# Graph attention: value aggregation one quad later and split between the score products, K|V buffers returned tile by tile

## The chip, the core and the metric

The kernel runs on one core of a Trainium2 chip. The metric is the device time of one execution in microseconds (us). TensorE does the matrix products (PE in the profile, its weight loads PEld), VectorE is DVE, ScalarE is ACT, GpSimd is POOL and SyncE is SP. The DMA engines move data between memory (HBM) and the on-chip buffers, and they are started here by SP (plain copies) and by POOL (gathers and scatters by index).

## The reference, cut to what matters

A graph of 3125 nodes with 512 features and 53125 edges, sorted by target node. After a layer norm the kernel computes two graph-attention layers, a linear-attention branch on the same input, and a mixture of eight small feed-forward experts. The change touches the attention over edges, which runs once in each of the two layers:

```python
q = ((x @ Wq[l].T + bq[l]) * scaling).reshape(n, H, DH)     # H = 8 heads, DH = 64
k = (x @ Wk[l].T).reshape(n, H, DH)
v = (x @ Wv[l].T).reshape(n, H, DH)
scores = jnp.einsum('ehd,ehd->eh', q[tgt], k[srcidx])
m = segment_max(scores, tgt); p = jnp.exp(scores - m[tgt]); s = segment_sum(p, tgt)
agg = segment_sum((p / (s[tgt] + 1e-16))[:, :, None] * v[srcidx], tgt)
```

## The kernel before

**Tiles, quads, groups.** The edges are padded to 416 tiles (`ET`) of 128. Four tiles are a quad, 104 quads (`NQ`); two quads are a group of eight tiles, 52 groups (`NJ`). Within a tile at most 16 different target nodes occur (`CAP` slots), and eight heads times 16 slots give 128 columns.

**What one quad needs.** POOL gathers, for every tile, the 128 rows of K|V (4 KB each, 512 KB in all) by source index into one of `KVN` = 20 buffers in layer 0 and 25 in layer 1 (`fetch`, line 1096). For every group it gathers the Q rows (`fetch_slots`, line 1105) and writes the 128 aggregated rows back by index (`scatter`, line 1113). So POOL starts five indexed DMAs in a quad: four `fetch`, and a `fetch_slots` or a `scatter` in turn. All are issued one after another on the one POOL queue, in the order of the program, and each waits for its semaphores there.

TensorE, per iteration `g` of the loop in `attend_pe`:

1. `turn_k` (line 1179): transposes K of four tiles, two ahead (`LOOK`), four 128x128 transposes for a tile. It waits for the tile's K|V DMA. ACT (line 1346) and DVE (line 1284) copy the results out of PSUM.
2. `turn_hot` (line 1160) in even iterations, `turn_q` (line 1171) in odd ones.
3. `turn_p` (line 1186): transposes the probabilities of quad `g - 2`; DVE copies them into `probs` (line 1272).
4. `masks` (line 1197): four bf16 products that start the score bank of the quad.
5. `score` (line 1209) for four tiles: for each tile four products, each with 32 weight columns, into partitions 0 to 31, 32 to 63, 64 to 95 and 96 to 127 (the columns of the array in four strips). The last one of a tile increments the semaphore `sc`. After the fourth tile DVE takes the minimum over the bank (line 1277) and ACT the exponentials (line 1365, one iteration later).
6. `gather` (line 1221) of quad `g - AGG_AT`, `AGG_AT` = 2: for each of the eight heads a product for each of the four tiles, with 32 weight columns from `probs` and V of the tile as the moving operand. Tile `i` goes to strip `i` of the bank `AG`. The very last product increments `agg`.

The profile's records show a product of fp32 operands in `score` and `gather` as two, so 32 records of line 1209 and 64 of line 1221 stand for a quad.

**What `agg` releases.** POOL's `fetch` of tile `n` waits until the quad that holds tile `n - KVN` is aggregated; `empty_p` on DVE waits for it before it overwrites `probs`; `empty_agg` on DVE (line 1297), once for a group, copies the bank `AG` out, increments `ev`, and `scatter` waits for `ev`. In layer 0 TensorE, DVE and ACT also do the output of the linear-attention branch in between (`side`; lines 743 to 796 on TensorE and DVE): these generators are advanced at four points of an iteration, and none lies between `score` and `gather`. Layer 1 has no such side work.

The order of the instructions on every engine is fixed by these loops and by the list that `turn_table` writes; nothing is reordered by a planner.

Of the kernel before, what the change touches and what calls it, by code (L numbers as in the profile page):

```python
# [7 lines left out]
N, D, H, DH = 3125, 512, 8, 64  # L8
# [5 lines left out]
ET = 416  # L14
# [14 lines left out]
LOOK = (2, 2)  # L29
AGG_AT = 2  # L30
FAR = 8192.0
# [49 lines left out]
def build(nc, A, out):  # L81
    with ExitStack() as ctx:
# [744 lines left out]
        def turn_table(l):  # L827
# [3 lines left out]
            for g in range(NQ + AGG_AT):  # L831
                b, x = divmod(g, 2)
                order += [("k", n) for n in range(4 * g + LOOK[l], 4 * g + LOOK[l] + 4) if n < ET]
                if x == 0 and b + 2 < NJ:
                    order.append(("hot", b + 2))
                if x == 1 and b + 1 < NJ:
                    order.append(("q", b + 1))
                if g >= AGG_AT:
                    order.append(("p", g - AGG_AT))
            place, by, count = {}, [], {"a": 0, "d": 0}  # L840
# [14 lines left out]
        def place_of(l, kind, n):  # L855
            return TURNED_AT[l][0][kind, n]
# [227 lines left out]
        def attend_pool(l, begin):  # L1084
# [7 lines left out]
            def fetch(n):  # L1092
                a = n % KV
                if n >= KV:
                    pool.wait_ge(agg, NQ * l + (n - KV) // 4 + 1)
                pool.indirect_dma_start(out=kvs[a], out_offset=None, in_=KVd[l][:, :],  # L1096
# [36 lines left out]
            at = KV  # L1133
            for g in range(NQ + AGG_AT + 2):
                j = (g + 3) // 2
                if g % 2 and j < NJ:
                    fetch_slots(j)
                x = (g - 2 - AGG_AT) // 2
                if g % 2 == AGG_AT % 2 and 0 <= x < NJ:
                    scatter(x)  # L1140
                while at < ET and (at - KV) // 4 <= g - AGG_AT:
                    fetch(at)
                    at += 1

        def attend_pe(l, side):
# [66 lines left out]

            def gather(g):
                x = g % 2
                is_emptied(pe, l, place_of(l, "p", g))
                if x == 0 and g:
                    pe.wait_ge(ev, NJ * l + g // 2)
                for h in range(H):
                    for i in range(4):
                        a = (4 * g + i) % KVN[l]  # L1220
                        mm = pe.matmul(AG[32 * i:32 * i + 32, DH * h:DH * (h + 1)], probs[x][:, i, h, :],  # L1221
                                       kvs[a][:, D + DH * h:D + DH * (h + 1)], start=(x == 0 and h == 0), stop=(x == 1),
                                       skip_group_check=True)
                mm.then_inc(agg, 1)
# [11 lines left out]
            for g in range(NQ + AGG_AT):  # L1236
# [9 lines left out]
                if x == 1 and b + 1 < NJ:  # L1246
                    turn_q(b + 1)
                if g >= AGG_AT:
                    turn_p(g - AGG_AT)
                next(side, None)  # L1250
                if g < NQ:
                    masks(g)
                    for i in range(4):
                        score(4 * g + i)
                if g >= AGG_AT:
                    gather(g - AGG_AT)
                next(side, None)

        def attend_dve(l, side, begin, work_free):
# [7 lines left out]
            def empty_p(g):  # L1267
                x = g % 2
                bank = bank_of("p", g)
                if g >= 2:  # L1270
                    dve.wait_ge(agg, NQ * l + g - 1)
                dve.tensor_copy(probs[x][:, :, :, CAP * x:CAP * (x + 1)],  # L1272
# [20 lines left out]
            def empty_agg(j):  # L1293
                dve.wait_ge(agg, NQ * l + 2 * j + 2)
                if j or l:
# [20 lines left out]
            for g in range(NQ + AGG_AT):  # L1316
# [5 lines left out]
                if x == 0 and b + 2 < NJ:  # L1322
                    empty_hot(l, b + 2)
                if g >= AGG_AT:
                    empty_p(g - AGG_AT)
                next(side, None)
# [62 lines left out]
        def edges_done(e, l):  # L1389
            e.wait_ge(agg, NQ * (l + 1))  # L1390
            e.wait_ge(ev, NJ * (l + 1))
# [1267 lines left out]
```

## Time and profile before

| | |
|---|---|
| median of 3 runs | 3487.64 us (3484.23 to 3498.01) |
| profiled execution | 3486.91 us, span 3485.6 us |
| PE busy | 2825.2 us (81%) |
| PEld busy | 2291.8 us (66%) |
| DVE, ACT, POOL busy | 1626.5, 1323.0, 1161.3 us (47%, 38%, 33%) |
| chain that ended last | PE 75%, issue 12%, DVE 8%, DMA 2%, ACT 2% |
| mean granted TensorE clock | 0.918 of full speed |

A record of a matmul has a start that is measured and an end that is modelled. "issue" is time in which an engine waited for nothing that the profile can name, and "remote" is a releaser that it can't name. Attention of layer 0 lies at about 512 to 1425 us of the span, that of layer 1 at about 1880 to 2781 us.

### The profile page before, as it was taken

The page shows a single profiled execution, that of the slowest core. Times are in us where ns is not written, and L with a number is a line of the kernel's source. Part 1 is how long each engine was busy: PE and PEld are TensorE (multiplying, and loading weights), DVE is VectorE, ACT ScalarE, POOL GpSimd, SP SyncE. Part 2 cuts the span into 40 slices and gives each one's busy share as a digit, 9 for nine tenths or more (in the row PEclk, how much of TensorE's full clock was granted, in tenths as well). Part 3 has the DMA queues.
Part 4 walks back from the last instruction along what each step waited for, and adds up shares of the span by engine and source line. Part 5 has one row for each costly group of instructions (what it writes and reads, how often), then busy time and mean ns, then how long its engine had stood idle before and what let it go on. Part 6 is the DMA issues. An engine that isn't in the chain of part 4 may idle for free.

```text
span 3485.6 us, 78342 instructions
## 1 busy us (share of the span) xinstructions
PE 2825.2 (81%) x32605; PEld 2291.8 (66%) x32605; DVE 1626.5 (47%) x3272; ACT 1323.0 (38%) x3690; POOL 1161.3 (33%) x1130
## 2 busy tenths in 40 slices
PE   6999978888888888587996777777777758588888
PEld 5877866666676676464885666666666646366676
DVE  5247764444444444547123333333443455655443
ACT  3324434444444444322322344444444412243333
POOL 0000015555555555100012555655565401312110
PEclk8999989999999999789998899998988979799989
DMA  6531037887888888430234777777777642022211
GB/s 215 218 139 68 28 127 237 264 268 264 269 269 273 266 270 270 109 117 0 91 148 147 253 260 263 268 261 258 264 261 259 184 114 72 25 78 89 64 52 53
DMA packets 231795, 621.75 MB, mean 178 GB/s; under 512 B 39008, under 2 KB 45792, under 8 KB 231427
## 3 DMA queue, kind: packets, MB, share of 16 engines
q0 software_dynamic: 137088, 466.78, 40.1%
q1 hardware_dynamic: 94339, 149.78, 12.9%
q8 instruction: 265, 4.34, 0.5%
q14 instruction: 103, 0.84, 0.1%
HBM read 538.80 MB, written 103.39 MB: 184 GB/s over the span
## 4 chain that ended last, share of the span: by engine, by line
PE 75%; issue 12%; DVE 8%; DMA 2%; ACT 2%; another core or an unknown queue 1%; POOL 0%; SPq 0%; POOLq 0%; DVEq 0%; ACTq 0%
PE ps L1179 12%; PE ps L1221 9%; PE ps L1209 6%; PE ps L574 4%; PE ps L576 4%; PE ps L575 4%; PE ps L1186 3%; PE ps L774 3%; PE ps L942 2%; PE ps L944 2%; PE ps L943 2%; PE ps L1867 2%; PE ps L1171 1%; PE ps L1869 1%; PE ps L1868 1%
## 5 line engine op out<-in xcount | busy, mean ns | idle before, releaser
L1096 POOL DMA_INDIRECT Y<-KVd,srcE x449 | 457.2, 1018 | 374.9 <-PE ps L1221 237.8
L1277 DVE TENSOR_REDUCE stage<-ps 128x4 f32<-128x512 f32 x208 | 143.8, 692 | 629.8 <-remote 501.1
L1346 ACT ACTIVATE work<-ps 128x512 f32<-128x512 f32 x309 | 179.7, 597 | 506.8 <-PE ps L1179 472.3
L1221 PE MATMUL ps<-Y,G 128*32 128x64 f32 x7184 | 237.7, 226 | 161.9 <-issue 158.9
L1346 ACT ACTIVATE G<-ps 128x512 f32<-128x512 f32 x315 | 182.1, 598 | 421.8 <-PE ps L1179 388.4
L1096 POOL DMA_INDIRECT WA<-KVd,srcE x186 | 188.6, 1014 | 419.4 <-PE ps L576 266.3
L1221 PEld LDWEIGHTS ps<-Y,G 128*32 128x32 f32 x7184 | 181.9, 112 | 207.2 <-issue 202.7
L1365 ACT ACTIVATE stage<-ps,stage 128x128 f32<-128x128 f32 x832 | 294.0, 366 | 35.0 <-PE ps L1186 27.1
L1179 PE MATMUL ps<-ident,Y 128*128 128x128 f32 x1796 | 261.3, 303 | 2.6 <-issue 1.4
L574 PE MATMUL ps<-Wh,xs 128*128 128x512 f32 x600 | 239.0, 398 | 29.9 <-DVE xs L514 29.8
L1179 PEld LDWEIGHTS ps<-ident,Y 128*128 128x128 f32 x1796 | 231.9, 158 | 29.3 <-issue 21.0
L576 PE MATMUL ps<-Wh,xs 128*128 128x512 f32 x600 | 236.7, 395 | 0.0
L575 PE MATMUL ps<-Wl,xs 128*128 128x512 f32 x600 | 236.5, 394 | 0.0
L1272 DVE COPY G<-ps 128x512 f32<-128x512 f32 x208 | 143.8, 691 | 165.3 <-PE ps L1186 136.0
L1105 POOL DMA_INDIRECT stage<-Qd,segs x104 | 105.9, 1018 | 330.8 <-DVE segs L893 195.3
L514 DVE TENSOR_TENSOR xs<-xT,xs 128x512 fp32r<-128x512 f32 (+1 forms) x100 | 67.8, 679 | 235.3 <-ACT xs L539 235.3
L1096 POOL DMA_INDIRECT mt<-KVd,srcE x54 | 53.8, 997 | 357.4 <-DMA Qd<-stage 319.7
L1365 ACT ACTIVATION_READ_ACCUMULATOR stage<-ps,stage 128x1 f32 x832 | 169.2, 203 | 0.0
L1221 PE MATMUL ps<-WA,G 128*32 128x64 f32 x2976 | 101.2, 230 | 68.4 <-issue 67.3
L574 PEld LDWEIGHTS ps<-Wh,xs 128*128 128x128 f32 x600 | 113.1, 188 | 56.5 <-issue 23.2
L1291 DVE TENSOR_TENSOR stage<-stage,st 128x512 f32<-128x512 f32 x208 | 143.9, 692 | 7.1
L2567 PE MATMUL ps<-W2hi,workR 128*128 128x512 f32 (+1 forms) x200 | 94.6, 473 | 58.4 <-DVE mtR L2614 58.4
(383 smaller groups left out, 6950.0 us busy)
## 6 DMA issues: line engine op xcount, KB each, us to landing
KVd<-stage SPq DMA_DIRECT2D x96, 256.0 KB, 2.0
aggd<-work SPq DMA_DIRECT2D x6, 2048.0 KB, 7.4
Qd<-stage SPq DMA_DIRECT2D x48, 256.0 KB, 2.0
G<-aggd SPq DMA_DIRECT2D x48, 256.0 KB, 2.7
Y<-KVd,srcE POOLq DMA_INDIRECT x449
Y<-in_x SPq DMA_DIRECT2D x4, 1536.0 KB, 15.0
G<-mixq SPq DMA_DIRECT2D x24, 256.0 KB
mixd<-rowsb SPq DMA_DIRECT2D x24, 256.0 KB
```

Of the source, the lines that this page charges most:

```text
L574: pe.matmul(PS[e % 4][0:r, :], xh, Wh[:, w, k, :], start=(k == 0), stop=False)
L575: pe.matmul(PS[e % 4][0:r, :], xh, Wl[:, w, k, :], start=False, stop=False)
L576: mm = pe.matmul(PS[e % 4][0:r, :], xl, Wh[:, w, k, :], start=False, stop=(k == 3))
L1096: pool.indirect_dma_start(out=kvs[a], out_offset=None, in_=KVd[l][:, :], in_offset=bass.IndirectOffsetOnAxis(ap=srcE[:, n:n + 1], axis=0)) ...
L1179: mm = pe.transpose(bank[:, k * P:(k + 1) * P], kvs[a][:, k * P:(k + 1) * P], ident[:, :])
L1209: mm = pe.matmul(bank[32 * k:32 * k + 32, at], qblk[j % 2][:, k, 2 * (c % 4) + c // 4, :], kT[n % len(kT)][:, k * P:(k + 1) * P], start=Fa ...
L1221: mm = pe.matmul(AG[32 * i:32 * i + 32, DH * h:DH * (h + 1)], probs[x][:, i, h, :], kvs[a][:, D + DH * h:D + DH * (h + 1)], start=(x == 0 ...
L1272: dve.tensor_copy(probs[x][:, :, :, CAP * x:CAP * (x + 1)], bank[:, :].rearrange("p (c h s) -> p c h s", c=4, h=H)).then_inc(out_d, 1)
L1277: dve.tensor_reduce(smin[:, 4 * g:4 * g + 4], SC[g % 2][:, :].rearrange("p (c e) -> p c e", c=4), AXX, ALU.min).then_inc(mins, 1)
L1291: dve.tensor_tensor(p4, p4, rec4[:, :].unsqueeze(2).to_broadcast([P, 4, P]), ALU.mult).then_inc(normed, 1)
L1346: act.activation(kT[n % len(kT)], banks(l)[place_of(l, "k", n) % len(banks(l))][:, :], ACT.Copy).then_inc(out_a, 1)
L1365: last = act.activation(pT[g % len(pT)][:, P * i:P * (i + 1)], SC[g % 2][:, P * i:P * (i + 1)], ACT.Exp, bias=smin[:, t:t + 1], scale=-1.0 ...
```

## The change

`gather` takes the tile as a second argument. It now does the eight products of one tile and increments `agg` once for every tile. The loop of TensorE calls it behind each `score`, so an iteration does score, gather, score, gather and so on; and the quad that is aggregated is the one three back (`AGG_AT` = 3), while its probabilities are still transposed two iterations after the scores (`P_AT` = 2). Every wait on `agg` counts tiles instead of quads. `fetch` of tile `n` waits for tile `n - KVN` alone. In POOL's loop `scatter` now stands ahead of `fetch_slots`, and with `AGG_AT` odd both fall into the odd iterations. The loops have one more iteration in each attention. The number of products, copies and DMAs is the same.

```diff
--- before.py
+++ after.py
@@ -27,7 +27,7 @@
 CAP = 16
 MASK = 2.0 ** 100
 LOOK = (2, 2)
-AGG_AT = 2
+P_AT, AGG_AT = 2, 3
 FAR = 8192.0
 BIG = 1.0e30
 EPS = 1e-5
@@ -835,8 +835,8 @@
                     order.append(("hot", b + 2))
                 if x == 1 and b + 1 < NJ:
                     order.append(("q", b + 1))
-                if g >= AGG_AT:
-                    order.append(("p", g - AGG_AT))
+                if 0 <= g - P_AT < NQ:
+                    order.append(("p", g - P_AT))
             place, by, count = {}, [], {"a": 0, "d": 0}
             for e, (kind, n) in enumerate(order):
                 who = "d" if kind in ("hot", "p") or kind == "k" and n % 4 == K_DVE[l] else "a"
@@ -1092,7 +1092,7 @@
             def fetch(n):
                 a = n % KV
                 if n >= KV:
-                    pool.wait_ge(agg, NQ * l + (n - KV) // 4 + 1)
+                    pool.wait_ge(agg, ET * l + n - KV + 1)
                 pool.indirect_dma_start(out=kvs[a], out_offset=None, in_=KVd[l][:, :],
                                         in_offset=bass.IndirectOffsetOnAxis(ap=srcE[:, n:n + 1], axis=0)
                                         ).then_inc(kv_in[a], 16)
@@ -1132,12 +1132,12 @@
                 fetch(n)
             at = KV
             for g in range(NQ + AGG_AT + 2):
+                x = (g - 2 - AGG_AT) // 2
+                if g % 2 == AGG_AT % 2 and 0 <= x < NJ:
+                    scatter(x)
                 j = (g + 3) // 2
                 if g % 2 and j < NJ:
                     fetch_slots(j)
-                x = (g - 2 - AGG_AT) // 2
-                if g % 2 == AGG_AT % 2 and 0 <= x < NJ:
-                    scatter(x)
                 while at < ET and (at - KV) // 4 <= g - AGG_AT:
                     fetch(at)
                     at += 1
@@ -1210,17 +1210,16 @@
                                    kT[n % len(kT)][:, k * P:(k + 1) * P], start=False, stop=True, skip_group_check=True)
                 mm.then_inc(sc, 1)
 
-            def gather(g):
-                x = g % 2
-                is_emptied(pe, l, place_of(l, "p", g))
-                if x == 0 and g:
-                    pe.wait_ge(ev, NJ * l + g // 2)
+            def gather(g, i):
+                x, a = g % 2, (4 * g + i) % KVN[l]
+                if i == 0:
+                    is_emptied(pe, l, place_of(l, "p", g))
+                    if x == 0 and g:
+                        pe.wait_ge(ev, NJ * l + g // 2)
                 for h in range(H):
-                    for i in range(4):
-                        a = (4 * g + i) % KVN[l]
-                        mm = pe.matmul(AG[32 * i:32 * i + 32, DH * h:DH * (h + 1)], probs[x][:, i, h, :],
-                                       kvs[a][:, D + DH * h:D + DH * (h + 1)], start=(x == 0 and h == 0), stop=(x == 1),
-                                       skip_group_check=True)
+                    mm = pe.matmul(AG[32 * i:32 * i + 32, DH * h:DH * (h + 1)], probs[x][:, i, h, :],
+                                   kvs[a][:, D + DH * h:D + DH * (h + 1)], start=(x == 0 and h == 0), stop=(x == 1),
+                                   skip_group_check=True)
                 mm.then_inc(agg, 1)
 
             if l == 0:
@@ -1245,15 +1244,16 @@
                     turn_hot(b + 2)
                 if x == 1 and b + 1 < NJ:
                     turn_q(b + 1)
-                if g >= AGG_AT:
-                    turn_p(g - AGG_AT)
+                if 0 <= g - P_AT < NQ:
+                    turn_p(g - P_AT)
                 next(side, None)
                 if g < NQ:
                     masks(g)
-                    for i in range(4):
+                for i in range(4):
+                    if g < NQ:
                         score(4 * g + i)
-                if g >= AGG_AT:
-                    gather(g - AGG_AT)
+                    if g >= AGG_AT:
+                        gather(g - AGG_AT, i)
                 next(side, None)
 
         def attend_dve(l, side, begin, work_free):
@@ -1268,7 +1268,7 @@
                 x = g % 2
                 bank = bank_of("p", g)
                 if g >= 2:
-                    dve.wait_ge(agg, NQ * l + g - 1)
+                    dve.wait_ge(agg, ET * l + 4 * (g - 1))
                 dve.tensor_copy(probs[x][:, :, :, CAP * x:CAP * (x + 1)],
                                 bank[:, :].rearrange("p (c h s) -> p c h s", c=4, h=H)).then_inc(out_d, 1)
 
@@ -1291,7 +1291,7 @@
                 dve.tensor_tensor(p4, p4, rec4[:, :].unsqueeze(2).to_broadcast([P, 4, P]), ALU.mult).then_inc(normed, 1)
 
             def empty_agg(j):
-                dve.wait_ge(agg, NQ * l + 2 * j + 2)
+                dve.wait_ge(agg, ET * l + 4 * (2 * j + 2))
                 if j or l:
                     dve.wait_ge(sct, 16 * (NJ * l + j))
                 dve.tensor_copy(stage[:, 0, :], AG[:, :]).then_inc(ev, 1)
@@ -1321,8 +1321,8 @@
                 next(side, None)
                 if x == 0 and b + 2 < NJ:
                     empty_hot(l, b + 2)
-                if g >= AGG_AT:
-                    empty_p(g - AGG_AT)
+                if 0 <= g - P_AT < NQ:
+                    empty_p(g - P_AT)
                 next(side, None)
                 if g < NQ:
                     least(g)
@@ -1387,7 +1387,7 @@
                 next(side, None)
 
         def edges_done(e, l):
-            e.wait_ge(agg, NQ * (l + 1))
+            e.wait_ge(agg, ET * (l + 1))
             e.wait_ge(ev, NJ * (l + 1))
 
         def edges_stored(e, l):
```

## Rows read from the trace of the kernel before

**Rows 1.** Windows: attention of layer 0 and of layer 1, and the opening of layer 1's.

```profile
core 0: us, PE busy (x) PEld busy (x) DVE busy (x) ACT busy (x) POOL busy (x), PEclk, DMA share, GB/s
520.00:1385.00 865.00, 731.12 (x12807) 594.99 (x12805) 396.05 (x883) 391.06 (x1227) 494.82 (x481) 0.97 0.80 265
1920.00:2757.00 837.00, 634.48 (x11881) 561.14 (x11874) 327.33 (x630) 363.66 (x1163) 488.24 (x484) 0.89 0.78 260
...
1886.90:1902.30 15.40, 5.37 (x32) 2.65 (x22) 0.29 (x1) 0.52 (x1) 9.47 (x11) 0.66 1.00 380
```

**Rows 2.** Chain of waits in layer 1, two quads: start us, us, what.

```profile
2182.16 3.51 PE ps L1179 x16
...
2186.44 1.01 PE ps L1209 x32
...
2189.71 1.02 PE ps L1221 x55
2190.74 1.90 PE ps L1179 x16
...
2193.73 1.01 PE ps L1209 x32
...
2198.29 0.91 PE ps L1221 x47
2199.19 0.40 PE ps L1179
```

**Rows 3.** Timeline of POOL over the same two quads.

```profile
2182.44 1.30 POOL L1096 DMA_INDIRECT rowsb<-KVd,srcE  x1 [2.13 <-PE ps L1221]
...
2187.77 1.00 POOL L1113 DMA_INDIRECT aggd<-stage,segs  x1 [0.30 <-issue]
2191.01 1.29 POOL L1096 DMA_INDIRECT WA<-KVd,srcE  x1 [2.24 <-PE ps L1221]
...
2196.33 1.02 POOL L1105 DMA_INDIRECT stage<-Qd,segs  x1 [0.30 <-issue]
```

**Rows 4.** Timeline of DVE over the same two quads.

```profile
2189.97 0.69 DVE L1277 TENSOR_REDUCE stage<-ps 128x4 f32<-128x512 f32 x1 [3.03 <-remote]
```

**Rows 5.** Chain of waits near the end of layer 1's attention, no fetches left.

```profile
2763.56 1.01 PE ps L1209 x32
2764.57 0.89 PE ps L1221 x64
2765.47 1.90 PE ps L1179 x16
...
2769.24 0.11 issue
```

**Rows 6.** Timeline of POOL near the end of layer 1's attention.

```profile
2768.05 0.99 POOL L1113 DMA_INDIRECT aggd<-stage,segs  x1 [10.88 <-DVE stage L1297]
```

**Rows 7.** Timelines of POOL and of DVE, opening of layer 1's attention.

```profile
1886.06 0.94 POOL L1096 DMA_INDIRECT Y<-KVd,srcE  x1 [0.31 <-issue]
...
1898.48 0.94 POOL L1096 DMA_INDIRECT rowsb<-KVd,srcE  x1 [0.31 <-issue]
...
1902.62 0.69 DVE L1277 TENSOR_REDUCE stage<-ps 128x4 f32<-128x512 f32 x1 [14.12 <-remote]
```

**Rows 8.** Chain of waits in layer 0, first and last row of four quads.

```profile
1005.25 1.01 PE ps L1209 x32
...
1039.94 0.23 PE ps L1209
```

**Rows 9.** Windows: the rest of these four quads, outside score and gather, summed.

```profile
sum 19.35, PE 18.73 PEld 15.28 DVE 10.98 ACT 9.86 POOL 14.47; mean PE 4.68 PEld 3.82 DVE 2.75 ACT 2.46 POOL 3.62
```

**Rows 10.** Chain of waits at the end of layer 0's attention.

```profile
1405.76 7.09 DMA Y<-KVd,srcE
```

**Rows 11.** Chain of waits in layer 0, a change from score to gather.

```profile
927.52 0.04 PE ps L1221 x3
927.56 0.01 PE ps L1209
927.57 0.94 PE ps L1221 x60
```

## The prediction, made before the run

> **What bounds the kernel now.** I read the page first and then split the span into stretches; both attentions together are half of it. In layer 0 and in layer 1 alike PE is busy for 85% and 76% of the time, DMA for 80% and 78%, POOL for 57% and 58% [rows 1]. None of them is full, so the bound is a loop. The chain of waits shows it. In layer 1 two quads take 2199.19 - 2182.16 = 17.03 us, 8.52 us a quad, and the 32 records of the scores are through in 1.01 us, but the mass of the gather follows only 2.3 and 3.6 us later, with PE waiting for nothing the profile can name [rows 2]. The stall is real, not one of recording: DVE, which needs only the last score, starts its minimum at 2189.97, 0.26 us after the gather moves again [rows 4].
>
> The timeline of POOL tells what the stall follows. A train of five indexed DMAs starts at 2182.44 and its last issue ends at 2188.77; PE moves again at 2189.71, 0.94 us behind it. The next train starts at 2191.01 and ends at 2197.35; PE moves at 2198.29, again 0.94 us behind [rows 2, 3]. From the first issue to the release are 7.27 and 7.28 us, 1.455 us for each DMA. Two counterproofs stand in the same trace. Near the end, where no fetch is left, the scores and the gather of a quad take 2765.47 - 2763.56 = 1.91 us and there is no stall; one lone scatter issued at 2768.05 ends a little stall that lasts to 2769.35, 1.30 us from its issue [rows 5, 6]. At the opening of layer 1, POOL issues eleven fetches in a row from 1886.06, and DVE waits 14.12 us for the first quad's scores, until 1902.62: 16.56 us, 1.51 us for each DMA [rows 7]. So products on 32-column strips (scores and gather) hardly complete while POOL issues indexed DMAs, whereas the transposes of line 1179 go on beside them: 16 in 1.90 us, the pace of the quad without fetches [rows 2, 5].
>
> The loop of a quad is therefore: gather done, 0.27 us, five DMAs at 1.455 us each (7.27), release, the rest of the scores and the gather (about 0.95), together 8.5 us. The transposes lie under the train. Layer 0 runs at (1039.94 - 1005.25) / 4 = 8.67 us a quad [rows 8].
>
> **The change part by part.** Products, copies and DMAs are the same in number, so only waits move. A release by tile lets POOL start its train inside the stretch of scores and gathers, where the train does its harm.
>
> (a) Layer 1. Let PE be free to work on strips at T. A tile's score and gather take 1.91 / 4 = 0.48 us [rows 5]. POOL's first fetch starts at T + 0.48 + 0.27 = T + 0.75. How soon it stops PE the trace bounds: not before 0, and behind the lone scatter PE still took in records until 2769.24, 1.19 us after its issue [rows 5, 6]; I take 0.5 us, nearer to 0 because records are queued before they are executed. By T + 1.25 two to three tiles are gathered, and their fetches make a train of three: 3 x 1.455 = 4.37, release at T + 5.12. The fourth tile ends at T + 5.60. The rest of the quad (transposes and masks) takes 2193.73 - 2190.74 = 2.99 and 2186.44 - 2182.16 = 4.28 us, the second at the lower granted clock; mean 3.64 [rows 2]. Sum 9.24 us. The fourth fetch lies under that rest. In every second iteration scatter and slots come behind it: 0.27 + 3 x 1.455 = 4.64 us, 1.0 more than the rest covers, 0.5 a quad. Together 9.75 us against 8.52: +1.23 us, times 104 quads +128 us.
>
> (b) Layer 0, the same loop. The rest of a quad is 19.35 / 4 = 4.84 us because of the side work [rows 9], which covers those three DMAs: 5.60 + 4.84 = 10.44 us.
>
> (c) Layer 0, K|V buffers. With 20 of them and the gather three back, buffers free after iteration g - 1 allow fetches up to tile 4g + 7, and `turn_k` of iteration g wants tile 4g + 5 at once (with two back: 4g + 11). So the second fetch released by one iteration is needed at the start of the next. It is issued 0.75 + 1.30 + 0.30 = 2.35 us after T [rows 3]; the chain shows 7.09 us from such an issue to the data [rows 10], so tile 4g + 5 can be turned at T + 9.44. Its transposes (1.90 / 4 = 0.48) and what follows them until the scores (2.99 - 1.90 = 1.09) [rows 2] come behind: 11.0 us. Bounds: 7.09 was behind other fetches, so 11.0 is an upper end; the lower end is nothing, where 10.44 of (b) stays. I take 10.6 us: 10.6 - 8.67 = +1.93, times 104 quads +201 us. In layer 1 with 25 buffers the allowance is 4g + 12, seven tiles to spare, no cost.
>
> (d) Taken away: the gather no longer waits for DVE's copy of the same iteration's probabilities. That copy runs beside the scores, and the stall behind them is longer than it; worth nothing. POOL's new order puts `scatter` and `fetch_slots` behind one another: the wait of `fetch_slots` for `turn_q` now has nothing behind the scatter to fill it, and the fetches of the iteration stand behind it in POOL's queue; they need gathers that come later anyway. Between 0 and one DMA (1.455 us) in every second quad of layer 0, where side work makes `turn_q` late; I take 0 and keep 52 x 1.455 = 76 us for the range. `empty_agg` and `ev` move with the gather and are awaited an iteration's transposes later: nothing.
>
> (e) One more iteration in each attention and a first refill one quad later: about 4 us each, +8 us, an estimate from half a quad; between 0 and 2 x 9.
>
> Sum: 128 + 201 + 8 = +337 us. The profiled execution took 3486.91 us (span 3485.6), within 1 us of the median, 3487.64. 3487 + 337 = 3824; I say 3825 us.
>
> **Rules of the skill.** The row first: near 927.5 us three records of the gather stand ahead of the last record of the scores [rows 11], so products on other strips pass one that is held, and I let the eight products of one tile, all on one strip, overlap with the next tile's scores. The Trainium skill ("TensorE: Matmul & The Clock Gate", Part 3: Packing small matmuls) says that matmuls start and end strictly in program order. By that rule they would run one behind another, the serial rival below. The skill ("SBUF — State Buffer", SBUF: two separate sides) also says that engine ports and DMA ports can't disturb each other and that TensorE waits for nobody there. By that the stall would have another cause, and the faster rival below would be the likelier. Rows 7 speak against it.
>
> **Rivals.**
>
> Serial strips. A tile's 16 gather records on one strip take as long as 64 on four, 0.89 us [rows 5], so a tile costs 0.89 + 0.25 = 1.14. After a gather PE has 0.27 + 0.5 us before the fetch stops it, less than a tile: every tile pays its own DMA. The next tile does 0.77 of its 1.14 us, waits for the release 0.27 + 1.455 = 1.73 after that gather and ends 0.37 later: 2.1 us a tile, the fourth at T + 7.4. A quad takes 7.4 + 3.64 + 0.5 = 11.5 us in layer 1 (+3.0) and 7.4 + 4.84 = 12.2 in layer 0 (+3.6), 104 x 6.6 = 686 us: 4170 us. For it speaks that the products are on one strip; against it rows 11.
>
> Faster: POOL's issues don't stop PE when strip work comes in small pieces. Then layer 1 is bound by POOL's train, five issues, 2196.33 + 1.02 + 0.30 - 2191.01 = 6.64 us a quad [rows 3]: -1.88 x 104 = -196 us. Layer 0 keeps (c), whose loop without the stall is 0.48 + 0.27 + 1.60 + 7.09 + 1.57 = 11.0 us at most and what it is now at least: 0 to +240, middle +100 (nearer to the lower end, since 7.09 is an upper one). About 3390 us. It decides if a quad's strip work in layer 1 ends less than about 3 us after it began although POOL is issuing. Against it: every one of the trains above.
>
> Same: the fetches collect into one train as before and the data of (c) arrive early; 3495 us.
>
> Only (c): the stall is no longer than before in either layer and only layer 0 pays: 3487 + 201 = 3690 us.
>
> **How the numbers follow.** The loop of (a) to (c) 0.50, serial strips 0.20, only (c) 0.07, same 0.09, faster 0.14. The likeliest gives 3825 us, its own range 3640 (onset at 1.2 us, so that all tiles are through in layer 1) to 4000 (76 us of (d), and a lower clock for the transposes in every quad, 104 x 0.9). The range given goes down to 3470, which takes in the same case, and up to 4250, which takes in the serial strips: outside it are the faster case (0.14) and a few hundredths above. Half a per cent, 17 us, is about what a measurement of this kernel can tell from no change; faster by more than that 0.14, within it 0.09, slower 0.77.
>
> **What the profile after would show.** If right: two stalls in each iteration between records of lines 1209 and 1221, each about 0.9 us behind the end of a POOL issue; POOL idle before fetches twice in a quad rather than once, with 1221 as releaser; about 9.7 us a quad in layer 1 and 10.6 in layer 0, there with line 1179 waiting for K|V DMAs; DMA in layer 1 at 260 x 8.52 / 9.75 = 227 GB/s. Serial strips would show as 16 records of line 1221 spread over 0.9 us even where POOL is idle. The prediction is wrong if the strips' work proceeds beside POOL's issues: a quad of layer 1 then falls below 8 us.

## The result and the profile after

Before 3492.82 us (median of 4 runs, 3484.23 to 3501.8), after 3780.09 us (4 runs, 3769.35 to 3783.95): 1.0817 times, 95% interval 1.0779 to 1.0856. The change makes the kernel 287 us slower, +8%; predicted were 3825 us (3470 to 4250). The profiled execution took 3769.35 us, its span is 3768.0 us, 282 more than the span before.

Where the time went is quickly told by line 1197, of which each quad has four products: the first and the last start of its rows, 103 quads apart, give the mean quad. Here is the view of line 1197 by attention, of before and then of after (count, durations, first and last start in us):

```profile
L1197 PE MATMUL ps<-hotTs,maskA x416: 216/219/229, 520.3 to 1417.6; 128*128 128x128 bf16 x139
L1197 PE MATMUL ps<-hotTs,maskA x416: 219/219/311, 1886.0 to 2771.8; 128*128 128x128 bf16 x139
```

```profile
L1197 PE MATMUL ps<-hotTs,maskA x416: 218/219/315, 520.5 to 1665.4; 128*128 128x128 bf16 x139
L1197 PE MATMUL ps<-hotTs,maskA x416: 218/219/314, 2139.9 to 3044.0; 128*128 128x128 bf16 x139
```

Layer 0 goes from 8.71 to 11.12 us a quad, 104 x 2.41 = 250 us; layer 1 from 8.60 to 8.78, 104 x 0.18 = 19 us. The rest, 13 us, lies around the attentions. So nearly all of it is layer 0, while I had expected 128 us of it in layer 1.

The page after, to set beside the table of before, and its windows, one for each attention (columns as in [rows 1]):

```profile
PE 3184.1 (85%) x32605; PEld 2662.0 (71%) x32605; DVE 1612.9 (43%) x3272; ACT 1317.1 (35%) x3690; POOL 1127.9 (30%) x1130
...
PE 60%; DMA 12%; DVE 10%; another core or an unknown queue 8%; issue 5%; ACT 2%; POOL 1%; SPq 1%; DVEq 0%; POOLq 0%; ACTq 0%
```

```profile
520.00:1664.00 1144.00, 971.70 (x13296) 845.41 (x13296) 404.71 (x907) 413.64 (x1274) 489.82 (x495) 0.96 0.64 207
2140.00:3043.00 903.00, 794.89 (x12403) 711.44 (x12402) 332.61 (x658) 370.73 (x1227) 491.69 (x501) 0.99 0.78 252
```

PE is busy for 359 us more than the 2825.2 of before, with the same 32605 records: the same work is now wider in time. DMA stands in the chain with 12% instead of 2%. (The 8% with an unnamed releaser lie mostly in layer 1; the piece at 2203.79, 6.43 us long, is DVE's minimum waiting for the scores of its quad.) In layer 0 the chain of waits shows why (start us, us, what):

```profile
1011.33 0.35 PE ps L1209 x8
1011.68 0.82 PE ps L1220 x15
...
1014.52 0.26 issue
1014.77 5.37 DMA Y<-KVd,srcE
...
1020.29 1.08 PE ps L1179 x4
...
1022.76 1.71 PE ps L774 x2
...
1028.79 5.37 DMA Y<-KVd,srcE
...
1034.29 0.63 PE ps L1179 x4
...
1039.15 5.56 DMA Y<-KVd,srcE
```

One turn of the loop is read off it: the second tile's gather ends at 1014.52, 0.26 us later its fetch starts, 5.37 us later the data are there, the transposes of that one tile, the side work (line 774) and the rest follow, then the scores and two gathers, and the next fetch of the same kind starts at 1028.79, 14.02 us after the last. The next turn takes 10.36 us. That is step (c) of the prediction. It does not bind every turn: from 530 to 1640 us, about 100 turns, the chain passes through 67 such DMAs (median 5.45 us), and the mean turn is 11.12 us. Two more things are to be seen. Fifteen or sixteen records of line 1220 take 0.82 to 0.9 us each time, as long as the 64 of a whole quad before, 0.89 us [rows 5]: the products of one strip run one behind another, 0.056 us apart. And behind the first of these waits PE works at the lower clock: four transposes take 1.08 us there and 0.63 in the second turn. The windows give the granted clock in the last column but two, 0.50 of full speed (the 1.2 GHz level). This is the rare case: over layer 0 the mean is 0.96, against 0.97 before [rows 1]. The window behind the first wait:

```profile
1020.30:1024.80 4.50, 4.50 (x17) 3.10 (x17) 1.31 (x5) 2.10 (x9) 0.00 (x0) 0.50 0.32 127
```

In layer 1 PE waits for no K|V data. The timeline of PE (start us, us, line, count, idle before) over most of a quad, and that of POOL:

```profile
2203.18 1.00 PE L1220 MATMUL ps<-Y,G 128*32 128x64 f32 x15
...
2205.10 0.80 PE L1209 MATMUL ps<-work,qblk 128*32 128x128 f32 x6
2206.22 0.40 PE L1220 MATMUL ps<-Y,G 128*32 128x64 f32 x4 [0.32 <-issue]
2206.98 0.46 PE L1220 MATMUL ps<-Y,G 128*32 128x64 f32 x5 [0.35 <-issue]
2207.70 0.38 PE L1220 MATMUL ps<-Y,G 128*32 128x64 f32 x4 [0.26 <-issue]
...
2208.23 1.06 PE L1220 MATMUL ps<-Y,G 128*32 128x64 f32 x16
```

```profile
2201.59 1.21 POOL L1096 DMA_INDIRECT Y<-KVd,srcE  x1 [1.04 <-PE ps L1220]
2203.40 1.01 POOL L1113 DMA_INDIRECT aggd<-stage,segs  x1 [0.60 <-PE ps L1186]
2204.71 1.03 POOL L1105 DMA_INDIRECT stage<-Qd,segs  x1 [0.30 <-issue]
2206.05 0.96 POOL L1096 DMA_INDIRECT Y<-KVd,srcE  x1 [0.31 <-issue]
```

The stall is there, but it is not a full stop: from 2206.22 to 2208 the products come four or five at a time, 0.72 to 0.76 us apart. And POOL's issues stand in shorter trains. If an idle time over 0.5 us is counted as a break, layer 1 of before (1920 to 2757 us) has 96 trains, each of five, as in [rows 3]; after (2180 to 3000 us) it has 183 single issues, 65 trains of two, 49 of three and one of five.

### The profile page after: what moved, and what is told of

The parts are those of the page before. It is cut to its first block, busy times and chain, and to the rows that moved or that the text cites. A ratio compares the mean times of both kernels' runs of the same rounds, so it can differ in the third digit from the quotient of the medians.

```text
span 3768.0 us, 78342 instructions
## 1 busy us (share of the span) xinstructions
PE 3184.1 (85%) x32605; PEld 2662.0 (71%) x32605; DVE 1612.9 (43%) x3272; ACT 1317.1 (35%) x3690; POOL 1127.9 (30%) x1130
## 4 chain that ended last, share of the span: by engine, by line
PE 60%; DMA 12%; DVE 10%; another core or an unknown queue 8%; issue 5%; ACT 2%; POOL 1%; SPq 1%; DVEq 0%; POOLq 0%; ACTq 0%
PE ps L1220 11%; DMA Y<-KVd,srcE 6%; PE ps L1179 5%; PE ps L1209 5%; PE ps L574 4%; PE ps L575 4%; PE ps L576 4%; PE ps L1186 3%; DMA G<-KVd,srcE 2%; PE ps L942 2%; PE ps L944 2%; PE ps L943 2%; DMA WA<-KVd,srcE 2%; PE ps L774 2%
## 5 line engine op out<-in xcount | busy, mean ns | idle before, releaser
L1096 POOL DMA_INDIRECT Y<-KVd,srcE x449 | 438.0, 976 | 499.2 <-PE ps L1220 325.8
L1220 PE MATMUL ps<-Y,G 128*32 128x64 f32 x7184 | 487.6, 221 | 31.3 <-issue 30.4
L1220 PEld LDWEIGHTS ps<-Y,G 128*32 128x32 f32 x7184 | 455.1, 112 | 49.5 <-issue 48.5
L1179 PE MATMUL ps<-ident,Y 128*128 128x128 f32 x1796 | 243.0, 278 | 90.8 <-DMA Y<-KVd,srcE 80.2
L1179 PEld LDWEIGHTS ps<-ident,Y 128*128 128x128 f32 x1796 | 199.6, 143 | 132.3 <-issue 76.7
L1220 PE MATMUL ps<-WA,G 128*32 128x64 f32 x2976 | 200.6, 220 | 13.3 <-issue 13.0
L1220 PEld LDWEIGHTS ps<-WA,G 128*32 128x32 f32 x2976 | 187.5, 111 | 19.1 <-issue 18.9
L1186 PE MATMUL ps<-ident,stage 128*128 128x128 f32 x832 | 137.8, 291 | 26.9 <-ACT G L1346 7.0
```

The source lines that it names most:

```text
L1179: mm = pe.transpose(bank[:, k * P:(k + 1) * P], kvs[a][:, k * P:(k + 1) * P], ident[:, :])
L1186: mm = pe.transpose(bank[:, i * P:(i + 1) * P], pT[g % len(pT)][:, i * P:(i + 1) * P], ident[:, :])
```

## The experiments

The kernels ran in three groups, each beside runs of the kernel before on the same chip: e1 to e4 (before: 3131.65 us), e5 to e8 (3473.49 us), e9 to e12 (3492.54 us). The first group's chip ran the kernel before 10% faster than the others; what was seen of that chip is told in the last section. us a quad is read from line 1197 as above. The first group's chip has no profile of before; its layer 0 stands in e2 (7.39 us) and its layer 1, unchanged, in e1 (6.45).

| kernel | times before, interval | layer 0, us a quad | layer 1 |
|---|---|---|---|
| e1 before, 16 buffers in layer 0 | 1.173, 1.168 to 1.177 | 12.70 | 6.45 |
| e2 after, layer 0 as before | 1.026, 1.021 to 1.030 | 7.39 | 7.16 |
| e3 three back, whole | 1.172, 1.167 to 1.177 | 12.61 | 6.44 |
| e4 three back, parts by heads | 1.168, 1.163 to 1.173 | 12.48 | 6.43 |
| e5 before | 1.000, 0.998 to 1.002 | 8.60 | 8.53 |
| e6 after | 1.083, 1.080 to 1.087 | 11.26 | 8.67 |
| e7 two back, parts by tile | 1.053, 1.050 to 1.057 | 10.26 | 8.61 |
| e8 two back, parts by heads | 1.029, 1.026 to 1.032 | 9.00 | 9.06 |
| e9 two back, tile by tile at the end | 1.060, 1.056 to 1.063 | 10.11 | 9.13 |
| e10 after, 20 buffers in layer 1 | 1.141, 1.138 to 1.143 | 11.22 | 10.73 |
| e11 before, half rows | 0.994, 0.992 to 0.996 | 8.61 | 8.53 |
| e12 after, release by quad | 1.253, 1.249 to 1.256 | 15.08 | 10.65 |

### The look-ahead alone: e1, e3, e4, e10

e1, on the kernel before:

```diff
-KVN = (20, 25)
+KVN = (16, 25)
```

> The kernel before with 16 instead of 20 K|V buffers in layer 0: same order, same products, but the same look-ahead as after the change (buffers free after iteration g-1 allow fetches up to tile 4g+7). Theory supply (layer 0's loss is the short look-ahead, the data of tile 4g+5 come too late): the release comes at the end of the gather, the second fetch is issued 0.27 + 1.27 us later, its data 5.4 us after that, then transposes, side work, masks, scores and gather (about 5 us): 12 us a quad instead of 8.7 in layer 0, 3490 + 104 x 3.3 = 3830 us. Rival order (layer 0's loss comes from products in series on one strip and from the stalls that they meet): nothing of that is changed here, 3490 us.

Measured 3675.36 us, 12.70 us a quad in layer 0 against 7.39: +5.3. The products, their order and the number of DMAs are those of before; only the look-ahead is that of after. Two turns in e1's chain of waits:

```profile
1195.38 5.37 DMA Y<-KVd,srcE
...
1209.06 5.13 DMA WA<-KVd,srcE
...
1219.86 0.90 POOL G L1096
1220.76 0.45 issue
1221.21 5.30 DMA G<-KVd,srcE
```

The turns take 13.68 and 12.15 us, of which 5.1 to 5.4 are a fetch's way from issue to data; in the second, 1.35 more are the first fetch, which stands ahead of the one that is needed. The expectation had been reckoned on the slower chip's time before. The quad came out near it, 12.70 for 12 us, but the loss did not: +5.3 us for +3.3, 1.173 times for 1.10.

A part of the 5.3 us is the clock. Layer 0 without and with the short look-ahead on this chip, e2 and then e3, which loses as e1 does:

```profile
530.00:1270.00 740.00, 671.09 (x13011) 570.04 (x13009) 402.23 (x890) 395.74 (x1245) 479.99 (x492) 0.98 0.89 314
530.00:1800.00 1270.00, 843.56 (x12944) 687.95 (x12943) 405.63 (x889) 406.26 (x1242) 494.18 (x490) 0.80 0.55 183
```

The mean granted clock is 0.80 instead of 0.98, and PE is busy for 843.56 instead of 671.09 us with about as many records (12944 and 13011). That is 1.7 us more a quad (1.8 in e1): PE waits for data, and then does the same work at the lower clock for part of the time.

e3 and e4, on the kernel after. e3:

```diff
                     if g < NQ:
                         score(4 * g + i)
-                    if g >= AGG_AT:
-                        gather(g - AGG_AT, i)
+                if g >= AGG_AT:
+                    gather_whole(g - AGG_AT)    # the loop over h, then i, of before; agg += 4
```

> The kernel after, but the gather stands whole at the end of the iteration, heads outermost (four strips in turn); it is still the quad three back. Theory supply: layer 0 has the look-ahead of e1 and its late release, 12 us a quad: 3830 us; layer 1 as before, 8.5. Rival order: without one-strip series both layers are as before, 3490 us.

e4:

```diff
-                for h in range(H):
-                    mm = pe.matmul(AG[32 * i:32 * i + 32, ...], probs[x][:, i, h, :], kvs[a][...], ...)
-                mm.then_inc(agg, 1)
+                for h in (2 * i, 2 * i + 1):
+                    for c in range(4):
+                        a = (4 * g + c) % KVN[l]
+                        mm = pe.matmul(AG[32 * c:32 * c + 32, ...], probs[x][:, c, h, :], kvs[a][...], ...)
+                if i == 3:
+                    mm.then_inc(agg, 4)
```

> The kernel after, but the four parts between the scores are two heads of all four tiles instead of eight heads of one tile; products alternate over four strips, and all four tiles are released at the last part. Theory supply: layer 0 like e3, 12 us a quad, 3830 us, layer 1 near 8.5 since the products go four abreast. Rival order (the series on one strip is the loss): near 3490 us. If parts of any kind between scores cost by themselves, layer 1 lies above 9 us a quad.

Both fall where e1 falls, 12.61 and 12.48 us in layer 0, and both leave layer 1 alone (6.44, 6.43). So neither the parts nor the series are needed to lose in layer 0; the third quad back with 20 buffers is enough. Both were run on the fast chip alone; how much the look-ahead alone costs on a chip of the slower kind, no run shows.

e10, on the kernel after:

```diff
-KVN = (20, 25)
+KVN = (20, 20)
```

> The kernel after with 20 instead of 25 buffers in layer 1, so that layer 1 has the look-ahead of layer 0 (up to tile 4g+7). Theory supply: line 1179 waits for K|V DMAs there too, a quad of layer 1 goes from 8.7 (or 7.2 without the stall) to about 10.5, the loop of layer 0 without its side work, and the whole 1.13 to 1.18 times before. Rival (layer 0 loses by its side work, not by the look-ahead): layer 1 stays, 1.083 times before where the stall is, 1.14 where it isn't.

Measured 3984.63 us, layer 1 at 10.73 us a quad. Its chain there, which has no side work, is the loop of layer 0:

```profile
2613.10 5.27 DMA mt<-KVd,srcE
...
2623.01 5.47 DMA WA<-KVd,srcE
```

Taking five buffers from layer 1 costs (10.73 - 8.67) x 104 = 214 us, with e6 on another chip of the slower kind for the 8.67. So the loss comes with the look-ahead of tile 4g + 7 and does not need the side work.

### The series on one strip: e2, e7, e9

e2, the kernel after with `AGG_AT` = 2 and the whole gather in layer 0, and the change in layer 1 only:

```diff
-P_AT, AGG_AT = 2, 3
+P_AT, AGGS = 2, (2, 3)          # AGGS[l] for AGG_AT throughout
...
-                    if g >= AGG_AT:
+                    if g >= AGGS[l] and not (l == 0):
                         gather(g - AGGS[l], i)
+                if g >= AGGS[l] and (l == 0):
+                    gather_whole(g - AGGS[l])
```

> The kernel after, but layer 0 gathers whole, two quads back, as before; layer 1 keeps the change. Theory supply: layer 0 goes back to 8.7 us a quad and layer 1 costs what the trace after shows, 8.78 - 8.60 = 0.18 us a quad, 19 us: 3510 us. My prediction's own step (a), a stall of three DMAs in each quad: +128 us, 3615 us.

Measured 3213.94 us, 82 us more than before on that chip. The expectation was written in the numbers of the result's chip; the test is the quad of layer 1, 7.16 us against 6.45: +0.7 us, where the result shows +0.18. The windows of e2 in layer 1 and its chain say what bounds it:

```profile
1760.00:2480.00 720.00, 712.64 (x12152) 690.41 (x12154) 333.43 (x646) 369.74 (x1201) 473.76 (x495) 1.00 0.90 312
```

```profile
2100.86 1.90 PE ps L1179 x16
...
2103.85 0.36 PE ps L1209 x8
2104.21 0.82 PE ps L1220 x15
...
2108.17 1.90 PE ps L1179 x16
```

PE is busy for 99% in the window, and the quad shown is 2108.17 - 2100.86 = 7.31 us without a gap. Scores and gathers take 4.32 of it, where the products over four strips took 1.91 [rows 5]. The series costs TensorE 2.41 us a quad. On this chip the quad of before has room for most of it, since POOL's issues set its 6.45 us (last section).

e7, on the kernel after:

```diff
-P_AT, AGG_AT = 2, 3
+P_AT, AGG_AT = 2, 2
```

> The kernel after with the quad two back instead of three (AGG_AT 2): parts, order and release by tile stay, the look-ahead of layer 0 is tile 4g+11 again. Theory supply alone: layer 0 falls back to what before takes, the whole to within 1% of before. Theory series and supply: layer 0 keeps the price of the series, four times 0.89 us of gather instead of 0.89, about +2.4 us a quad where TensorE is the bound (no stall: 7.36 + 2.4 = 9.8, together with 0.8 in layer 1 3131 + 104 x 3.2 = 3465 us, 1.106 times); on a chip with the stall the series lies partly under POOL's train: 9.5 to 10 us a quad, 1.03 to 1.04 times.

Measured 3662.52 us. With the look-ahead of before no wait of line 1179 for a DMA is left, and layer 0 falls from 11.26 to 10.26 us, not to 8.60. So of the 2.66 us that after loses in layer 0 on this chip, 1.00 goes with the look-ahead and 1.66 stays with parts and series. The split is rough: with the quad two back the gather waits for DVE's copy of the probabilities again, 13.6 us in e7's layer 0 (0.13 a quad), which after has not. The expectation of series and look-ahead together was right in kind and low in size (9.5 to 10 us a quad, 1.03 to 1.04 times). The windows of e7 in layer 0, first columns PE and PEld, show PE busy for 90% there:

```profile
530.00:1560.00 1030.00, 922.45 (x13007) 792.04 (x13006) 395.04 (x886) 397.25 (x1246) 493.83 (x492) 0.99 0.69 227
```

e9, on the kernel after:

```diff
-P_AT, AGG_AT = 2, 3
+P_AT, AGG_AT = 2, 2
...
                     if g < NQ:
                         score(4 * g + i)
+                for i in range(4):
                     if g >= AGG_AT:
                         gather(g - AGG_AT, i)
```

> Two back and all gathers behind the fourth score, as before, but tile by tile (eight heads of one tile, then the next) with release by tile: the series on one strip alone, with no score in between and no shorter look-ahead. Theory series: a gather of four tiles takes 4 x 0.9 us, 2.7 us more than over four strips; layer 0 at 10.0 to 10.5 us a quad as in e7 (10.26), the whole 1.05 to 1.07 times before on a chip with the stall, about 1.10 on a chip without. Rival (the parts between the scores are what costs, by breaking up the stretch): near before, within 1%.

Measured 3699.6 us, 10.11 us in layer 0. The series behind the scores, in one piece, costs 1.4 to 1.5 us in layer 0 (8.71 of the result's before, 8.60 of e5), most of the 1.66, so it is the series that costs and hardly the parts between the scores. In layer 1 it costs 0.6 us (9.13), more than with the parts (8.61); why it is more was not taken apart.

### Parts by heads without the third quad: e8

`AGG_AT` = 2 in the kernel of e4.

> Two back, four parts between the scores, each of two heads of all four tiles (four strips in turn), all four tiles released at the last part. Theory: neither the series nor the look-ahead is left of the change, so it is as fast as before within 1% on either kind of chip. If waiting for the copied probabilities of the same iteration costs, it shows here as up to 0.7 us a quad, 70 us.

Measured 3570.84 us, 97 us more than before: the "as fast as before" failed. The waits of PE (line, releaser: us in total, times, longest), first layer 0, then layer 1:

```profile
PE ps L1222 <- DVE G L1275: 65.7, 73, 2.9
...
PE ps L1222 <- issue: 172.3, 267, 1.2
PE ps L1222 <- DVE G L1275: 26.4, 86, 1.1
```

Line 1222 is the gather here, line 1275 DVE's copy of the probabilities. With the first part directly behind the first score, the gather waits for the copy of the same iteration, which the whole gather behind four scores hardly does: 3.1 us in the trace of before. The waits alone do not settle what it costs, since PE's unnamed waits before the gather became fewer at the same time (108.6 us in layer 0 of before, 19.2 in e8). The chain of waits does: the copy itself stands in e8's chain with 59.5 us from 530 to 1430 us and 58.6 from 1930 to 2850, 0.6 us a quad in each layer, and in e5's chain not once. Measured are +0.40 and +0.53 us a quad. So the rival named in the expectation, up to 0.7 us a quad, is the likely cause of the whole. Step (d), which I costed at nothing, is worth nothing against before, but the copy is what a split gather needs the third quad for.

### What stalls the strips: e5, e6, e11, e12

e5 and e6 are the two kernels unchanged.

> The kernel before, unchanged, for a profile on the chip that ran it in 3131 us or on one like the first (3487 us). The runs of e1 to e4 had quads of layer 1 in 6.4 us, which the loop that I read from the first trace (release only after a train of five POOL issues, 8.5 us) does not allow. Theory chip: where the time is near 3131 us the strip products go on beside POOL's issues (scores and gather of a quad in 1.9 us, quads of 7.3 us in layer 0 and 6.4 us in layer 1), and where it is near 3490 they stall (3.9 and 5.1 us). Rival: the stall is there in both, and the difference lies elsewhere in the span, outside the attentions.

> The kernel after, unchanged, on the same chip as e5. On a chip with the stall 1.08 times before. On a chip without it: layer 1 as in e2, 7.23 us a quad instead of 6.44 (the series on one strip makes TensorE the bound), layer 0 bound by the K|V loop of 11 us instead of 7.36: 3131 + 104 x (0.8 + 3.6) = 3590 us, 1.145 times. Rival: without the stall the loop of layer 0 shrinks as well, to 9.8 us: 3470 us.

Both landed on a chip of the slower kind (3471.26 and 3767.54 us) and repeat the first result: 1.083. For the fast chip there is thus no profile of before; e2 and e3 stand in for it below.

e11, on the kernel before:

```diff
-                pool.indirect_dma_start(out=kvs[a], out_offset=None, in_=KVd[l][:, :],
+                pool.indirect_dma_start(out=kvs[a][:, 0:D], out_offset=None,
+                                        in_=KVd[l].rearrange("n (a d) -> (n a) d", a=2),
...
-                                       kvs[a][:, D + DH * h:D + DH * (h + 1)], ...
+                                       kvs[a][:, DH * h:DH * (h + 1)], ...
```

> The kernel before with the same number of indexed DMAs, each moving 2 KB a row instead of 4: only the first 512 columns of a row (by the index of the other layout) are fetched, and the aggregation multiplies them instead of V. Theory issue: POOL's issues alone hold the strip products, 1.455 us for each, whatever they move: layer 1 stays at 8.5 us a quad on a chip with the stall (6.4 without), the whole within 2% of before. Rival bytes: the stall hangs on the traffic of the DMA engines (78% busy): layer 1 falls to 6.6 us a quad, POOL's five issues back to back, or less, and the whole to 0.92 or less on a chip with the stall.

This kernel leaves V out and multiplies the probabilities with what it fetched, so it computes something else and serves for its time alone. Measured 3471.87 us, layer 1 at 8.53 us a quad. Its windows in layer 1:

```profile
1930.00:2700.00 770.00, 585.60 (x10969) 521.56 (x10969) 301.56 (x584) 335.80 (x1070) 458.71 (x448) 0.90 0.49 140
```

The DMA engines are busy for 49% instead of 78% and move 140 GB/s instead of 260 [rows 1], and the quad does not move (e5: 8.53). The packets fell too, from about 650 to 400 a quad. So the stall does not hang on the bytes; what was kept is the five issues with 128 rows each.

e12, on the kernel after:

```diff
-                    pool.wait_ge(agg, ET * l + n - KV + 1)
+                    pool.wait_ge(agg, ET * l + 4 * ((n - KV) // 4 + 1))
```

> The kernel after with one change: a fetch waits until its whole quad is aggregated, so that all four come behind the last part. Theory: by-tile release helps layer 0, since the second fetch of an iteration, the one that turn_k waits for, goes about 2.2 us earlier (two parts of 1.1 us); without it 11.1 + 2.2 = 13.3 us a quad, the whole 1.083 + 0.065 = 1.15 times before where the stall is, and layer 1 within 0.3 us of after. Rival (my prediction's picture, where a release inside the stretch lets POOL's train stop it): layer 1 gets faster by 1 us a quad or more.

Measured 4375.99 us, the largest miss of the study: 15.08 us in layer 0 and 10.65 in layer 1. In layer 0 the chain gives 16.04 us from one awaited fetch to the next:

```profile
1208.46 5.00 DMA Y<-KVd,srcE
...
1222.88 1.31 POOL Y L1096
...
1224.50 5.16 DMA Y<-KVd,srcE
```

The fetch that is needed now stands behind all four parts and behind the first fetch. In layer 1 the fetches collect into trains again, and the serial products meet them in full. Chain and POOL's timeline:

```profile
2911.09 1.12 issue
...
2920.18 1.04 issue
```

```profile
2906.47 0.97 POOL L1096 DMA_INDIRECT Y<-KVd,srcE  x1 [5.23 <-PE ps L1220]
...
2915.37 1.28 POOL L1096 DMA_INDIRECT rowsb<-KVd,srcE  x1 [4.19 <-PE ps L1220]
```

POOL is idle for 4 to 5 us and then issues four to six times without a pause. The expectation, 13.3 us in layer 0 and layer 1 within 0.3 us of after, had left that out. So the release by tile is worth 2.0 us a quad in layer 1 and 3.8 in layer 0 once the products are in series: the opposite of what step (a) took it for.

## Why the prediction came out near, step by step

**The sum was near by luck, its terms were not.** Predicted +337 us, measured +287. Layer 0 was given 201 us and took 250; layer 1 was given 128 and took 19. The two errors have opposite signs and cancel for the most part.

**(a) Layer 1: this step failed.** It let three fetches stop the strips and put the transposes behind the end of the fourth tile. What the runs show in its place is a balance of three terms. The series adds 2.41 us of TensorE (e2: 4.32 against 1.91). The clock gives back 0.65: before, every second quad's rest took 4.28 us instead of 2.99 [rows 2], at a granted clock of 0.89 on average [rows 1], and after it is 0.99. (The transposes of line 1179, summed over these windows, take 2.70 us a quad before and 1.97 after.) And the stall shrinks. Before, 8.60 us less 1.91, 2.99 and 0.65 leaves 3.05 us of stall; after, 8.78 less the 7.31 of a quad without a gap leaves 1.47. These two are remainders and not measured by themselves. One reason is shown: the issues stand in shorter trains, and e12, which puts the long ones back, pays 2.0 us (0.2 of them in the transposes, at a granted clock of 0.89). Two more are seen in the trace, but no run prices them: held products still pass four or five at a time, and the end of the last tile is held while the transposes are already running. This last is seen around 2200 us, in the timelines of PE and of DVE and in the one of POOL above:

```profile
2198.80 0.38 PE L1209 MATMUL ps<-G,qblk 128*32 128x128 f32 x3
2198.94 1.06 PE L1220 MATMUL ps<-Y,G 128*32 128x64 f32 x16
2199.92 1.97 PE L1179 MATMUL ps<-ident,WA 128*128 128x128 f32 x16
```

```profile
2200.49 0.69 DVE L1277 TENSOR_REDUCE stage<-ps 128x4 f32<-128x512 f32 x1 [5.06 <-PE ps L1209]
```

The last score's record ends at 2199.18, but DVE, idle for 5.06 us, gets to its minimum only at 2200.49. The fourth tile's gather ends at 2200.00 in the records and the transposes begin at 2199.92, but the fetch that waits for that tile starts only at 2201.59, after 1.04 us of idle time. The ends of these records are modelled, and two engines that wait for them see them 1.3 to 1.6 us later. Near the end of the layer, where no fetch is left, the same minimum starts at 3041.77, 0.05 us behind the end of its last score.

**(b) Layer 0, 10.44 us a quad: the size is near what e7 shows (10.26), the reason was wrong.** It was reckoned as a stall of three DMAs; it is the series (e9 has it without parts and without the third quad, 10.11). That the two agree is luck.

**(c) The look-ahead: right in mechanism.** On the fast chip e1, e3 and e4 have it alone and lose 5.1 to 5.3 us a quad, with PE busy for 1.7 to 1.8 us more a quad at the lower clock; e10 carries it into layer 1. In after it adds about 1.00 us to the series: both share the loop, only about two turns in three wait for a DMA, and the clock hardly falls. The terms of my 11.0 were off both ways: issue to data takes 5.4 us, not 7.09; the fetch that is needed is issued 3.44 us after the scores' start (1011.33 to 1014.77), not 2.35, since the gathers ahead of it are in series; and behind the late transposes stands the side work (1.71 us in the turn shown), which I had left out. Measured are 11.12 us a quad, for 10.6 expected and 11.0 named as the upper end.

**(d)** Nothing against before, as said; the 76 us of POOL's order did not appear as a term of their own, and no run has that order alone. e8 shows the copy's cost, about 0.6 us a quad in the chain, where the split is made without the third quad. **(e)** +8 us stands against the 13 that lie outside the two attentions' quads.

**The rivals.** Serial strips is right in its mechanism: sixteen records on one strip take 0.82 to 0.9 us also while POOL is idle (15 in 0.82 us from 3038.57, with no issue of POOL between 3032.18 and 3044.68), as the prediction said they would show. The small passing of [rows 11], three records, is about all that products on other strips gain in the timelines above; I had built the overlap of a whole tile on it. The Trainium skill ("TensorE: Matmul & The Clock Gate", Part 3: Packing small matmuls) with its strict program order would have given the series, and the trace agrees with it to within a few records. The rival's price, 4170 us, was too high because it charged every tile a full DMA and added the transposes behind. The rival "only (c)" (3690) came nearest in layer 1, no loss for 19 us, though it named neither the series nor the shorter stall there, and its layer 0 lacked the series. The faster case is out on this chip: the stall persists, though smaller, and layer 1 stays above 8 us a quad. On the fast chip its condition, strip work that proceeds beside POOL's issues, is met (e2, 7.16 us); but there the kernel before has hardly a stall to lose either (6.45 us), and the series makes it slower.

**The signs named ahead:** line 1179 waits for K|V DMAs in layer 0 (right); 227 GB/s in layer 1 (252); 9.7 us a quad there (8.78); two stalls an iteration, each 0.9 us behind an issue (not so, it is a slow passing); POOL idle before fetches twice a quad (more often: of 371 fetches from 2180 to 3000 us, 266 have more than 0.5 us of idle time before them, nearly three in a quad).

## What to carry to other kernels

Count the buffers before you move a consumer back: one quad of delay took four of 20 buffers, and the loop through one fetch (issue to data 5.4 us, and all that must follow) became the bound in two turns of three, while 25 buffers hid it. When products on 32-column strips are reordered, keep neighbours on different strips; eight heads of one tile in a row took as long as 32 products over four strips. And when two effects share a loop, price each by a kernel that has it alone: the sum of mine came out near, with one term seven times too large.

## What was not expected of the hardware

**Chips of the same kind differ by 10% on this kernel.** 3131.65 us on one (3128.16 to 3151.79 in seven runs), 3473 to 3493 on the others. The fast chip was seen in this group of kernels only, so that it is the chip and not something else at that time is likely, but not shown. On the fast one, e2's serial gathers run at full pace beside POOL's issues, as in the chain above and this timeline of POOL over the same quad:

```profile
2103.01 1.01 POOL L1113 DMA_INDIRECT aggd<-stage,segs  x1 [0.30 <-issue]
...
2108.17 0.94 POOL L1096 DMA_INDIRECT Y<-KVd,srcE  x1 [0.30 <-PE ps L1220]
```

The quad in e3's layer 1, 6.44 us, is POOL's five issues back to back (6.64 us by [rows 3], 6.5 here: 463 issues in 600 us). The stall is not wholly absent there: e3's chain has single ones, one of 2.94 us from 2636.01 in a gather. The prediction had cited a rule here: engine ports and DMA ports can't contend (the Trainium skill, "SBUF — State Buffer", SBUF: two separate sides). e11 agrees with it, since half the bytes leave the quad at 8.53 us. The stall on the other chips then has another cause than that traffic, as the prediction allowed. [rows 7] show the stall but not where it arises, so they don't speak against the rule. Which chip a kernel lands on can't be chosen, so an absolute time, and even the balance between two schedules, must be compared on one chip: the whole change costs layer 1 0.7 us a quad on the fast one and 0.1 to 0.2 on the others.

**What stays open** is why the strips stall while transposes pass. e11 excludes the bytes; the trains and e12 tie it to POOL's issues standing close together, without showing that the issues and not something that goes with them are the cause. What of the issue reaches TensorE, and why one chip hardly has it, no run here shows.
